# A vision-transformer stack on one core: six phases in one order, the attention of one image pair beside the projection and MLP of the other pair

## The chip, the core and the metric

The kernel runs on one core of a Trainium2 chip. The metric is the device time of one execution in microseconds (us). Three executions of the kernel before gave a median of 682.43 us (679.1 to 685.9). A core has TensorE (PE, matrix products, results in PSUM), VectorE (DVE), ScalarE (ACT), GpSimd (POOL) and SyncE (SP), which here issues all DMAs. Each engine runs its own instructions in the order in which they were written; between engines there are only semaphores.

## The reference

Input: 4 images of 16 x 16 tokens with 192 channels, float32. Three transformer layers and a spectral layer follow each other:

```python
def layer(x):                      # layers 0, 1, 2
    y = layernorm(x)
    q, k, v = split(y @ wqkv + b)  # 12 heads
    s = q @ k.T * scale + rel_h(q) + rel_w(q)     # decomposed relative positions
    x = x + softmax(s) @ v @ wproj + bproj
    return x + gelu(layernorm(x) @ w1 + b1) @ w2 + b2   # 192 -> 768 -> 192
def spectral(x):                   # last
    f = rfft2(x); f = block_mlp(f)  # relu between, softshrink behind
    return irfft2(f) + x
```

Layers 0 and 2 have 12 heads of 16 channels and windows of 14 x 14: of an image, one window of 196 tokens is whole, and the 60 tokens at its edge lie in three windows filled up with padding tokens, whose keys and values count. Layer 1 has 12 heads of 48 channels over all 256 tokens of an image.

## The kernel before

It works on all four images (1024 tokens, eight tiles of 128 rows in X) and finishes a layer before the next begins: layernorm (DVE, the root on ACT), PE transposes into XT, q and k for 96 channels at a time, the relative terms, 12 heads of attention, projection, second layernorm, `up` with gelu on ACT, `down`, the next layer. The spectral layer closes it.

**One head.** Scores with position terms and masks are one product: SP builds for each head the operands QA and KA in a ring of slots (6 slots in layers 0 and 2, one tile of 128 rows; 4 slots in layer 1, two tiles), 3 or 6 DMAs per head (step `aug`: q with its rounding remainder, k, relative terms). Rows that never change (one-hot keys, masks) are laid once per layer (`load_constants`, L643). PE computes `max` units, DVE reduces them to row maxima, PE transposes the maxima (`maxT`), DVE copies them to NR, SP writes them into the last rows of QA (two DMAs, L726), and with them PE computes the transposed `scores` units, ACT takes the exponential into PT, PE multiplies by V into the O banks (`pv`), DVE and POOL divide.

**The order** is one list of steps, made by `all_steps`; every engine walks through it and issues what it has to do in each step, so the list fixes each engine's program and SP's queue. In `windowed_attention` (layers 0 and 2) and `whole_attention` (layer 1) maxima are taken ahead of the scores by some heads, the q, k and relative units of later chunks lie between the heads, and `attention_steps` adds projection and MLP at the end, with the second half of the images' layernorm beside the first half's products. All matmuls but the transposes go through one helper line, L1171, so operand names tell them apart: XT,WQKV (q, k), WQKV,XT (v), QD,RB and XNOS,RB (relative terms), QA,KA (maxima), KA,QA (scores), PT,V (pv), OT,WP (projection), XT,W (`up`), W,HT (`down`). An f32 matmul appears as two records in the trace. Layernorm in DVE's program:

```python
link(nc.vector.reciprocal(RSTD[:, 4 * u:4 * u + 4], STD[:, 4 * u:4 * u + 4]))
```

after ACT's square root of the variance (L859), which needs its own function table; so do exp and gelu.

Of the kernel before, what the change touches and what calls it, by code (L numbers as in the profile page):

```python
# [7 lines left out]
F32R = mybir.dt.float32r  # L23
ALU = mybir.AluOpType
# [6 lines left out]
TILES = NT // 128  # L31
CK = C // 2
HEADS, HALF = 12, 6
# [8 lines left out]
EDGES = 2 * BORDER  # L42
FIRST_EDGE = NB * INNER
PAD_KEYS = INNER - (IMG - EDGE) ** 2
FIRST_PAD = FIRST_EDGE + EDGES
PROBS = 2 * FIRST_EDGE + 2 * EDGES + 4 * EDGES
# [5 lines left out]
SHRINK = 0.01  # L52


class Layer:


    def __init__(self, index, head_dim, window, eps, gelu):
# [7 lines left out]

# [7 lines left out]
        self.npad = PAD_KEYS if self.pads else 0  # L74
        self.keys = NT + self.npad
        self.pc = self.npad // 2
        self.vtiles = 2 * NB + 2 if self.pads else TILES


        self.tiles = 1 if head_dim == 16 else 2  # L80
        self.ring = 6 if head_dim == 16 else 4
        parts = 2 if self.tiles == 1 else 1
        self.rel_row = 3 * head_dim if self.tiles == 1 else head_dim
        self.mask_row = self.rel_row + 2 * parts * window

        self.max_row = 126
        self.rows = 128
        self.depth = (self.rows,) * self.tiles
        self.aug_dmas = 3 if self.tiles == 1 else 6

        self.score_banks, self.unit_banks = ((2, 3, 4), (5,)) if self.tiles == 1 else ((2, 3), (4, 5))
        self.units = 6 if self.pads else 4
        self.pv_heads = 4 if self.pads else 2
        self.pv_steps = 5 if self.pads else 4
        self.max_units = 6 if self.pads else 4
        self.max_rows = 120 if self.pads else 128
        self.max_cols = 20 if self.pads else 16
        self.max_dmas = 2 if self.pads else 1
        self.per_pair = 4 if self.tiles == 1 else 8
# [3 lines left out]
          Layer(2, 16, 14, 1e-6, ACT.Gelu)]  # L103

# [6 lines left out]

def key_constants(L):

    w, parts = L.win, 2 if L.tiles == 1 else 1
    n = L.keys if L.pads else TOK
    hot = np.zeros((w, parts, 2, n), np.float32)
    masks = np.zeros((L.max_row - L.mask_row, n), np.float32)
    ones = np.ones((2, n), np.float32)

    def place(j, kh, kw):  # L120
        hot[w - 1 - kh, :, 0, j] = 1
        hot[w - 1 - kw, :, 1, j] = 1

    if not L.pads:
        for j in range(TOK):
            place(j, *divmod(j, IMG))
        hot = hot.transpose(2, 0, 1, 3)
# [3 lines left out]
    for b in range(NB):  # L131
        for i, (y, x, window) in enumerate(border()):
            j = edge_keys(b // 2).start + b % 2 * BORDER + i
            place(j, y % w, x % w)
            masks[b % 2 * 3 + window, j] = 1
    j = FIRST_PAD
    real = IMG - w
    for kh in range(w):
        for kw in range(w):
# [7 lines left out]
            j += 1  # L147
    return np.ascontiguousarray(np.concatenate([hot.reshape(-1, n), masks, ones]))


def query_masks():

    m = np.zeros((LAYERS[0].max_row - LAYERS[0].mask_row, NT), np.float32)
    for b in range(NB):
        for i, (_, _, window) in enumerate(border()):
            j = edge_queries(b // 2).start + b % 2 * BORDER + i
            m[:WINDOWS, j] = -BIG
            m[b % 2 * 3 + window, j] = 0
# [3 lines left out]


def edge_queries(k):
    return slice(FIRST_EDGE + k * EDGES, FIRST_EDGE + (k + 1) * EDGES)


def edge_keys(k):
    at = FIRST_EDGE + k * (EDGES + PAD_KEYS)
    return slice(at, at + EDGES)  # L170

# [5 lines left out]


def pad_keys_of(pc):
    half = PAD_KEYS // 2  # L180
    return slice(FIRST_PAD + pc * half, FIRST_PAD + (pc + 1) * half)
# [16 lines left out]
class Count:  # L198


    def __init__(self, nc, ctx, name, per_layer, step=1):
# [208 lines left out]
def _build(nc, ctx, io, out):  # L410
# [84 lines left out]
    def per(f):  # L495
        return [f(L) for L in LAYERS] + [0]
# [991 lines left out]
```

## Time and profile before

| what | value |
|---|---|
| median of three executions | 682.43 us (679.1 to 685.9) |
| profiled execution: span, instructions | 688.5 us, 9874 |
| PE busy | 590.2 us, 86% |
| DVE / ACT / POOL busy | 300.5 / 221.0 / 119.5 us |
| first scores of layer 0 | 54.2 us |
| scores of layer 0 end; its MLP ends about | 137; 202 us |
| layer 1: first maxima; scores | 237.7; 251 to 400.5 us |
| layer 2: scores | 503 to 585.6 us |
| spectral layer | 643 to 688.5 us |

PE's 86% is the busy time of pipelined matmuls at the clock they were granted; a stretch at half clock looks as busy as one at full clock with twice the work. The page's row PEclk, in tenths of full speed for 40 slices of 17 us, tells them apart. The chain of waits names, step by step back from the last instruction, what the time went to.

### The profile page before, as it was taken

The numbers are of one execution on the slowest core, as the hardware profiler recorded it, in microseconds if no ns is written. First come the engines' busy times: TensorE is split into PE (matmuls) and PEld (weight loads), VectorE is DVE, ScalarE is ACT, GpSimd is POOL, SyncE is SP. The second block draws the span as 40 slices with busy tenths as digits, with TensorE's granted clock in tenths as the row PEclk, the third lists the DMA queues.
The fourth block names the chain that finished last, engine by engine and source line by source line (L and its number), as shares of the span: only waits on it lengthen the run. The fifth ranks groups of instructions, "written<-read, shape, count | busy, mean of one in ns | idle before, by whom it ended". The sixth has DMA issues, their size and how long they took to land.

```text
span 688.5 us, 9874 instructions
## 1 busy us (share of the span) xinstructions
PE 590.2 (86%) x3696; PEld 431.0 (63%) x3696; DVE 300.5 (44%) x824; ACT 221.0 (32%) x437; POOL 119.5 (17%) x179
## 2 busy tenths in 40 slices
PE   7986778789989998898987899998876776999997
PEld 5655646674667666475755686666566465746777
DVE  4566628561133343344443544126566385510123
ACT  3314425524242133143342333134143255242120
POOL 5102001102003203050531114201020011030021
PEclk7897678788999999799999899999986788889999
DMA  5772433145215255408255232601623431120001
GB/s 154 179 153 55 94 78 64 39 110 123 59 36 127 41 112 126 101 1 170 60 111 120 50 96 67 150 11 33 139 69 79 89 69 38 35 59 0 1 0 47
DMA packets 21829, 54.13 MB, mean 79 GB/s; under 512 B 4642, under 2 KB 10522, under 8 KB 21686
## 3 DMA queue, kind: packets, MB, share of 16 engines
q1 hardware_dynamic: 21782, 53.50, 34.2%
q8 instruction: 30, 0.49, 0.3%
q14 instruction: 17, 0.14, 0.1%
HBM read 10.94 MB, written 0.79 MB: 17 GB/s over the span
## 4 chain that ended last, share of the span: by engine, by line
PE 64%; DVE 13%; SPq 9%; DMA 7%; issue 4%; ACT 3%; DVEq 0%; ACTq 0%
PE PS L1171 62%; DVE NM L1067 4%; DMA QA<-NR 4%; DMA QA<-REL 3%; SPq L704 3%; SPq L714 3%; PE PS L1187 2%; SPq L696 2%; SPq L726 1%; DVE REL L1054 1%; ACT REL L902 1%; DVE OT L1104 1%; DVE HL L1080 1%; DVE OT L1102 1%; DVE QHL L1035 1%
## 5 line engine op out<-in xcount | busy, mean ns | idle before, releaser
L1067 DVE TENSOR_REDUCE NM<-PS 98x2 f32<-98x392 f32 (+2 forms) x192 | 105.2, 569 | 109.3 <-PE PS L1171 107.2
L1171 PE MATMUL PS<-QA,KA 128*98 128x196 f32 (+2 forms) x480 | 103.8, 333 | 29.6 <-DMA QA<-NR 19.1
L1171 PE MATMUL PS<-KA,QA 126*98 126x196 f32 (+3 forms) x432 | 101.9, 336 | 28.8 <-DVE NM L1067 16.8
L922 ACT ACTIVATE PT<-PS 98x392 f32<-98x392 f32 (+2 forms) x192 | 94.2, 520 | 98.1 <-PE PS L1171 94.1
L1171 PEld LDWEIGHTS PS<-QA,KA 128*98 128x98 f32 (+2 forms) x480 | 80.6, 218 | 43.2 <-DMA QA<-NR 21.4
L1171 PEld LDWEIGHTS PS<-KA,QA 126*98 126x98 f32 (+3 forms) x432 | 69.5, 206 | 55.3 <-DVE NM L1067 28.2
L1171 PE MATMUL PS<-XT,W 96*128 96x512 f32 x144 | 70.0, 643 | 3.4 <-issue 3.4
L1171 PE MATMUL PS<-XT,WQKV 96*96 96x512 f32 x128 | 66.6, 654 | 4.7 <-issue 3.8
L1171 PE MATMUL PS<-PT,V 128*32 128x196 f32 (+2 forms) x672 | 56.8, 391 | 0.0
L1054 DVE TENSOR_TENSOR REL<-PS,REL 32x512 fp32r<-32x512 f32 (+5 forms) x64 | 28.4, 478 | 57.6 <-ACT REL L902 57.5
L1171 PE MATMUL PS<-W,HT 128*128 128x192 f32 x288 | 48.7, 328 | 4.7 <-ACT HT L943 4.7
L1171 PEld LDWEIGHTS PS<-W,HT 128*128 128x128 f32 x288 | 46.6, 190 | 9.6 <-ACT HT L943 9.6
L1171 PEld LDWEIGHTS PS<-XT,W 96*128 96x128 f32 x144 | 28.9, 206 | 37.6 <-issue 36.9
L823 POOL TENSOR_TENSOR OT<-XNOS,OT 128x512 f32<-128x512 f32 x18 | 22.8, 1274 | 151.2 <-DVE OT L1104 151.2
L902 ACT ACTIVATE REL<-PS 32x512 fp32r<-32x512 f32 (+5 forms) x64 | 25.1, 433 | 66.0 <-PE PS L1171 53.5
L1129 DVE TENSOR_TENSOR X<-X,PS 128x192 f32<-128x192 f32 x24 | 8.5, 354 | 84.7 <-PE PS L1171 84.7
L943 ACT ACTIVATE HT<-PS,COL 128x512 f32<-128x512 f32 x36 | 24.0, 685 | 53.4 <-PE PS L1171 53.4
L1171 PEld LDWEIGHTS PS<-XT,WQKV 96*96 96x96 f32 x128 | 21.6, 179 | 29.3 <-issue 29.2
L1171 PEld LDWEIGHTS PS<-PT,V 128*32 128x32 f32 (+2 forms) x672 | 27.5, 132 | 15.2 <-issue 2.5
L1171 PE MATMUL PS<-QD,RB 96*32 96x64 f32 x384 | 35.1, 253 | 1.5 <-DVE NR L1091 1.5
L1171 PEld LDWEIGHTS PS<-QD,RB 96*32 96x32 f32 x384 | 30.9, 117 | 6.9 <-DVE NR L1091 2.8
L804 POOL CAST QHL<-QD 96x1024 fp32r<-96x1024 f32 x6 | 6.2, 1035 | 154.6 <-ACT QD L882 90.5
(96 smaller groups left out, 674.7 us busy)
## 6 DMA issues: line engine op xcount, KB each, us to landing
QA<-QHL SPq DMA_DIRECT2D x36, 192.0 KB
KA<-KHL SPq DMA_DIRECT2D x24, 228.0 KB
QA<-REL SPq DMA_DIRECT2D x24, 224.0 KB
QA<-QHL SPq DMA_DIRECT2D x12, 384.0 KB
KA<-KHL SPq DMA_DIRECT2D x12, 384.0 KB
KA<-PT SPq DMA_DIRECT2D x12, 380.0 KB
W<-in_w SPq DMA_DIRECT2D x6, 576.0 KB, 5.2
QA<-REL SPq DMA_DIRECT2D x24, 128.0 KB
```

What stands on the lines that cost most here:

```text
L696: sp.dma_start(raw(dst), raw(src)).then_inc(aug_in[s].sem, 16)
L704: sp.dma_start(raw(dst), raw(src)).then_inc(aug_in[s].sem, 16)
L714: sp.dma_start(raw(dst), raw(src)).then_inc(aug_in[s].sem, 16)
L823: nc.gpsimd.tensor_tensor(o, OS[:, k, :], o, ALU.mult).then_inc(o_done.sem, 1)
L902: ins = nc.scalar.activation(dst, src, ACT.Copy)
L922: nc.scalar.activation(dst, src, ACT.Exp).then_inc(probs_done.sem, 1)
L943: nc.scalar.activation(m["HT"][:, i, u * 512:(u + 1) * 512], PS[:, bank, :], L.gelu, bias=COL[n][:, b1:b1 + 1]).then_inc(gelu_done.sem, 1)
L1054: ins = nc.vector.tensor_tensor(lo, src, hi.bitcast(F32), ALU.subtract)
L1067: nc.vector.tensor_reduce(dst, src, AX.X, ALU.max, negate=True).then_inc(max_done.sem, 1)
L1129: nc.vector.tensor_tensor(X[:, i, :], X[:, i, :], PS[:, bank, 0:C], ALU.add).then_inc(x_end.sem, 1)
L1171: return nc.tensor.matmul(dst, lhsT, rhs, start=start, stop=stop, skip_group_check=loose)
L1187: last = nc.tensor.transpose(PS[0:CK, bank + k, t * 128:(t + 1) * 128], XN[:, 4 * u + t, k * CK:(k + 1) * CK], IDN[:, :])
```

## The change

The images are split into two pairs (HB = 2), and the three layers into six phases, layer x pair: phase 0 and 1 are layer 0 of pairs 0 and 1, 2 and 3 layer 1, 4 and 5 layer 2. While the attention of phase p runs, unit by unit, the steps of `beside(p)` are put between its units: the tail of phase p-1 (projection, layernorm, `up`, gelu, `down`: the other pair) and the head of phase p+1 (layernorm, transposes, q, k, relative terms: again the other pair, next layer or same). They fill the first 75% of the attention's units (FILL). Each layer loads its weights once, in its first phase. Other edits go with it:

- Masks and operands are for two images; maxima are no longer split in two parts, one row (127) of QA holds them.
- Relative terms: per unit 64 matmuls of 32 x 32, to four column groups of PE in turn; 18 units in all, 2304 records instead of 640 records of 64 columns.
- Layernorm: 1/sqrt on DVE by an integer guess and three Newton steps, 12 small linked operations, instead of ACT's Sqrt and DVE's reciprocal.
- `up` leaves PSUM by an Identity on ACT; gelu then works in place over 128 x 1536, twice per phase, with one table load before it and one behind, inside the attention (13 loads in all, 6 before).
- PSUM: two banks for maxima, two for scores, one for O, three for everything beside (four, two and two before).
- At a change of layer kind (phase 1 to 2, 3 to 4) the constants of the ring (12 DMAs) are laid once all scores of the phase before are done, then `prelude`: the ring's `aug` DMAs (24, or 18) and the first heads' maxima, all ahead of the new phase's first scores.
- Matmul instructions go from 2370 to 3286, SP's DMAs from 280 to 481.

```diff
+def tail_steps(p):
+    out = [(("proj", 0, 0), 1.5), (("proj", 1, 0), 1.5), (("ln", 1, 0), 5.0), (("turn", 1, 0), 3.0)]
+    out += [(("up", m, 0), 1.5) for m in range(FM)]
+    out += [(("gelu", 0, 0), 0), (("gelu", 1, 0), 4.0)]
+    return out + [(("down", k, 0), 2.0) for k in range(2)]
...
+def beside(p):
+    out = []
+    if p:
+        out += [((p - 1, *step), d) for step, d in tail_steps(p - 1)]
+    if p % 2 == 0:
+        out.append(((p, "weights", 0, 0), 0))
+    if p == 5:
+        out += [((4, *step), d) for step, d in spectral_steps(0)]
+    if p + 1 < 6:
+        out += [((p + 1, *step), d) for step, d in head_steps(p + 1)]
+    return out
...
+FILL = [0.75] * 6
...
+def ordered():
+    out = [(0, *step) for step, _ in head_steps(0)]
+    out += prelude(0)
+    for p in range(6):
+        L = PHASES[p].L
+        if p and PHASES[p - 1].L is not L:
+            out += [(p, "constants", 0, 0), *prelude(p)]
+        out += second_chunk(p)
+        out += [(p, "v", t, 0) for t in range(L.vtiles)]
+        slots, extra = attention_slots(p), beside(p)
+        whole, at, placed = sum(d for _, d in extra) / FILL[p], 0.0, []
+        for step, d in extra:
+            placed.append((at / whole * len(slots), step))
+            at += d
+        for j, slot in enumerate(slots):
+            out += slot
+            while placed and placed[0][0] < j + 1:
+                out.append(placed.pop(0)[1])
+        out += [step for _, step in placed]
+        out += [(p, "pv", L.groups - 1, k) for k in range(L.pv_steps)] + [(p, "norm", 0, 0)]
+    out += [(5, *step) for step, _ in tail_steps(5)]
+    return out + [(5, *step) for step, _ in spectral_steps(1)]
...
+                link(nc.vector.tensor_scalar(VAR[:, :], MV[:, :, 1], L.eps, None, ALU.add))
...
+                for _ in range(3):
+                    link(nc.vector.tensor_tensor(SQ[:, :], RSTD[:, :], RSTD[:, :], ALU.mult))
+                    link(nc.vector.scalar_tensor_tensor(SQ[:, :], SQ[:, :], -0.5, VAR[:, :], ALU.mult, ALU.mult))
+                    link(nc.vector.scalar_tensor_tensor(RSTD[:, :], SQ[:, :], 1.5, RSTD[:, :], ALU.add, ALU.mult))
...
+            elif step == "constants":
+                sp.wait_ge(*scores_psum.at(p - 1, HEADS * PHASES[p - 1].L.units - 1))
+                lay_constants(ph)
+            elif step == "weights":
...
+                load_weights(L)
+                if p == 0:
+                    load_wqkv(1)
+                    for k in (1, 2):
+                        sp.dma_start(COL[k][:, :], io[f"col{k}"]).then_inc(col_in[k].sem, 16)
+                        load_columns(k)
...
+                for y in range(IMG):
+                    at = y % L.win
+                    for j in range(4):
+                        chunk, axis = divmod(j, 2)
+                        tokens, to = image(Q[rows, chunk, :]), image(PS[32 * j:32 * j + 32, bank[0], :])
+                        last = mm(to[:, :, :, y] if axis else to[:, :, y, :], RB[n][rows, axis, at:at + 16, :],
+                                  tokens[:, :, :, y] if axis else tokens[:, :, y, :], True, True)
```

**PE around the second layernorm of layer 0.** A row is one or several equal matmuls in PE's program: out<-weights,moving, rows x columns of it. Before, behind the projection (OT,WP), all images:

```order
L1171 MATMUL PS<-WP,OT 128x192 x24
L1187 MATMUL PS<-IDN,XNOS 96x128 x8
L1171 MATMUL PS<-XT,W_0 128x512 x4
L1187 MATMUL PS<-IDN,XNOS 96x128 x8
L1171 MATMUL PS<-XT,W_0 128x512 x8
L1171 MATMUL PS<-W_0,HT 128x192 x24
L1171 MATMUL PS<-XT,W_0 128x512 x12
L1171 MATMUL PS<-W_0,HT 128x192 x18
```

In the changed kernel, phase 1: the same layernorm (its transposes are IDN,XN x8, `up` is XT,W), with the attention of the other pair around it; the projection's second half (WP,OT x12) stands five rows above the first row:

```order
L1122 MATMUL PS<-QA,KA 98x196 x2
L1214 MATMUL PS<-IDN,NM 6x120
L1122 MATMUL PS<-KA,QA 98x196 x2
L1122 MATMUL PS<-QA,KA 98x196 x2
L1122 MATMUL PS<-KA,QA 98x196 x2
L1140 MATMUL PS<-IDN,XN 96x128 x8
L1122 MATMUL PS<-QA,KA 120x120 x3
L1122 MATMUL PS<-KA,QA 120x312
L1122 MATMUL PS<-QA,KA 98x196 x2
L1214 MATMUL PS<-IDN,NM 6x120
L1122 MATMUL PS<-KA,QA 98x196 x2
L1122 MATMUL PS<-XT,W 128x512 x2
```

Between the projection and the transposes lie 17 small attention matmuls (maxima QA,KA, scores KA,QA and one transpose of maxima), and between the transposes and the first `up` nine, where before the transposes followed the projection directly and `up` of the other half lay behind them.

**SP at the change from layer 0 to layer 1.** A row is one DMA. Before, behind the last rows of maxima (QA<-NR), while PE is at projection and MLP:

```order
L726 DMA QA<-NR 2x2x120
L731 DMA W_0<-in_w_0 96x1536
L732 DMA W_0<-in_w_0 128x1152
L641 DMA WQKV<-in_wqkv 96x3456
L673 DMA RB<-in_rb 96x124
L673 DMA VB<-in_vb 128x576
L673 DMA B_1<-in_b_1 128x192
L673 DMA COL<-in_col 128x26
L647 DMA KC<-in_kc 80x256
L658 DMA KA<-KC 80x4x256
L658 DMA KA<-KC 32x4x256
L662 DMA QA<-KC 46x4x256
```

In the changed kernel, behind the last rows of maxima of phase 1, with the first DMA waiting for the last scores:

```order
L676 DMA QA<-NR 1x15x8
L615 DMA KA<-KC 80x2x256
L615 DMA KA<-KC 32x2x256
L619 DMA QA<-KC 47x2x256
L615 DMA KA<-KC 80x2x256
L615 DMA KA<-KC 32x2x256
L619 DMA QA<-KC 47x2x256
L615 DMA KA<-KC 80x2x256
L615 DMA KA<-KC 32x2x256
L619 DMA QA<-KC 47x2x256
L615 DMA KA<-KC 80x2x256
L615 DMA KA<-KC 32x2x256
```

The weights are gone from this place, the constants have moved behind the last scores of the phase, and the `aug` DMAs of four heads follow them (six per head) before any maxima of layer 1.

**SP in phase 0.** In the changed kernel, from the row of head 2 (the first rows) on:

```order
L674 DMA QA<-NR 1x4x98
L676 DMA QA<-NR 1x15x8
L600 DMA WP<-in_wp 128x576
L601 DMA W<-in_w_0 96x1536
L602 DMA W<-in_w_0 128x1152
L591 DMA WQKV<-in_wqkv 96x3456
L693 DMA COL<-in_col 128x26
L594 DMA RB<-in_rb 96x124
L595 DMA VB<-in_vb 128x576
L596 DMA B_1<-in_b_1 128x192
L693 DMA COL<-in_col 128x18
L594 DMA RB<-in_rb 96x116
```

Behind these loads (ten of twelve are shown) stand, in the same queue, the operands of head 6 and the row of maxima of head 3. Before, the loads of the next layer stood behind the last rows of a layer's attention.

## Rows read from the trace of the kernel before

**Rows 1.** The page: span, busy time, and the granted TensorE clock in 40 slices
```profile
span 688.5 us, 9874 instructions
...
PE 590.2 (86%) x3696; PEld 431.0 (63%) x3696; DVE 300.5 (44%) x824; ACT 221.0 (32%) x437; POOL 119.5 (17%) x179
...
PEclk7897678788999999799999899999986788889999
```

**Rows 2.** Chain that ended last, shares of the span by engine
```profile
PE 64%; DVE 13%; SPq 9%; DMA 7%; issue 4%; ACT 3%; DVEq 0%; ACTq 0%
```

**Rows 3.** Stretches of 10 us: PE, PEld, DVE, ACT, POOL busy (instructions), granted clock, DMA
```profile
80.00:90.00 10.00, 2.34 (x17) 1.77 (x16) 3.33 (x11) 2.31 (x5) 0.00 (x0) 0.84 0.99 189
...
130.00:140.00 10.00, 7.99 (x57) 6.07 (x61) 1.89 (x8) 6.51 (x13) 1.26 (x1) 0.50 0.52 148
...
630.00:640.00 10.00, 9.22 (x32) 5.29 (x31) 0.34 (x1) 3.17 (x5) 0.00 (x0) 1.00 0.00 0
```

**Rows 4.** Timeline of PE: start, length, operation, count; dense work
```profile
170.74 8.07 PE L1171 MATMUL PS<-W,HT 128*128 128x192 f32 x48 [0.78 <-ACT HT L943]
178.64 10.46 PE L1171 MATMUL PS<-XT,W 96*128 96x512 f32 x24
...
215.60 8.76 PE L1171 MATMUL PS<-WQKV,XT 96*128 96x288 f32 x35
```

**Rows 5.** Timeline of PE: attention of layer 1 and of layer 2
```profile
262.80 1.08 PE L1171 MATMUL PS<-QD,RB 96*32 96x64 f32 x16
...
399.81 1.01 PE L1171 MATMUL PS<-QA,KA 128*128 128x256 f32 x7
400.75 3.67 PE L1171 MATMUL PS<-PT,V 128*64 128x256 f32 x32
...
545.15 0.40 PE L1171 MATMUL PS<-KA,QA 126*120 126x312 f32 x1
```

**Rows 6.** Timeline of PE: four narrow matmuls side by side
```profile
590.14 0.58 PE L1171 MATMUL PS<-PT,BV 96*32 96x120 f32 x16
590.56 0.38 PE L1171 MATMUL PS<-PT,V 120*32 120x120 f32 x8
590.76 0.58 PE L1171 MATMUL PS<-PT,BV 96*32 96x120 f32 x16
```

**Rows 7.** Chain, pieces in order of time (start, length): row of maxima, layer 0
```profile
81.92 1.10 SPq L696
...
83.08 1.36 SPq L704
...
84.53 0.83 SPq L714
...
85.42 0.72 SPq L726
...
86.19 4.29 DMA QA<-NR
...
133.19 1.65 DMA QA<-NR
```

**Rows 8.** Timeline of SP: constants laid into the ring's slots
```profile
21.54 0.81 SPq L654 DMA_DIRECT2D QA<-PT  x1
22.39 1.38 SPq L653 DMA_DIRECT2D KA<-PT  x1
```

**Rows 9.** Groups by shape on DVE and ACT: busy us, mean ns of one
```profile
L996 DVE TENSOR_SCALAR XNOS<-X,MV,RSTD 128x192 f32<-128x192 f32 x48 | 16.6, 409 | 0.4
...
L980 DVE BATCH_NORM_STATS2 STAT<-X 128x6 f32<-128x192 f32 x48 | 13.6, 345 | 3.1 <-DMA X<-in_x 3.1
...
L987 DVE RECIPROCAL RSTD<-STD 128x4 f32<-128x4 f32 x12 | 2.1, 178 | 27.7 <-ACT STD L859 27.7
...
L863 ACT ACT_TABLE_LOAD x6 | 7.7, 1283 | 0.1
```

**Rows 10.** DMA issues: KB each, median us to landing
```profile
WQKV<-in_wqkv SPq DMA_DIRECT2D x1, 1296.0 KB, 11.4
```

More of the change, by code:

```diff
@@ new lines, in attention_slots @@
+def attention_slots(p):
+    L = PHASES[p].L
+    slots = {(h, k): [(p, "scores", h, k)] for h in range(HEADS) for k in range(L.units)}
+    joined = p + 1 < 6 and PHASES[p + 1].L is L
+    for h in range(HEADS):
+        g, first = h // L.per_group, h % L.per_group == 0
+        if first and g:
+            for k in range(L.units):
+                slots[h, k].append((p, "pv", g - 1, k))
+            slots[h, L.units - 1].append((p, "copy_o", g - 1, 0))
+            slots[h + 1, 0].append((p, "inverse", g - 1, 0))
+            slots[h + 1, L.units - 1].append((p, "divide", g - 1, 0))
+        m = h + L.ahead
+        where = (p, m) if m < HEADS else (p + 1, m - HEADS) if joined else None
+        if where:
+            for k in range(L.units):
+                slots[h, k].append((where[0], "max", where[1], k))
+            late = (h + 1, 0) if h + 1 < HEADS else (h, L.units - 1)
+            slots[late].append((where[0], "maxT", where[1], 0))
+        a = h + L.ring
+        if a < HEADS:
+            slots[h, L.units - 1].append((p, "aug", a, 0))
+        elif joined and a - HEADS < L.ring:
+            slots[h, L.units - 1].append((p + 1, "aug", a - HEADS, 0))
+    if not L.pads:
+        for i in range(1, 3):
+            work = [(p, *step) for step, _ in unit_steps(i)]
+            at = range(0, 4) if i == 1 else range(4, 12)
+            for j, step in enumerate(work):
+                k = at[j * len(at) // len(work)]
+                slots[k // 2, k % 2].append(step)
+    return [slots[h, k] for h in range(HEADS) for k in range(L.units)]
@@ L405, in build, with all_steps @@
+BANKS = {"turn": 2, "q": 1, "k": 1, "rel": 1, "maxT": 1, "proj": 1, "up": 1, "down": 1, "fwd": 1, "s1": 1, "s2": 1,
+         "inv": 1}
+def all_steps():
+    taken = 0
+    for p, step, i, u in ordered():
+        n = BANKS.get(step, 0) if step != "v" else 1 if PHASES[p].L.pads else 2
+        banks = [DENSE[(taken + k) % len(DENSE)] for k in range(n)]
+        taken += n
+        yield PHASES[p], step, i, u, banks
 def build(nc, io, out):
@@ L582, in values, with split_free @@
+    def split_free(p, c):
+        L = PHASES[p].L
+        rooms = 1 if L.pads else 2
+        if c >= rooms:
+            return chunk_heads(p, c - rooms)
+        if not p:
+            return []
+        if new_layer(p):
+            return [wait for b in range(1, 3) for wait in chunk_heads(p - 1, PHASES[p - 1].L.chunks - b)]
+        return chunk_heads(p - 1, L.chunks - rooms + c)
     def values(L, t, h):
-        return mem[L.index]["V"][0:v_rows(L, t), t, h * L.vcol:h * L.vcol + L.slot]
+        rows = EDGES if L.pads and t == 2 * HB else 128
+        return V[L.index][0:rows, t, h * L.vcol:h * L.vcol + L.slot]
@@ L1207, in _ @@
+                        last = mm(PS[0:rows, bank[g], 0:wide], tokens, WQKV[n][:, k, cols], k == 0, k == 1)
                 last.then_inc(v_psum.sem, 1)
             elif step in ("q", "k"):
[L1209 to L1210 removed]
+                part = int(step == "k")
+                pe.wait_ge(*wqkv_in[n].at(0, 0))
                 permuted = part and L.pads
[L1212 removed]
```

1725 lines of the change are left out of this document (776 added, 949 removed).

## Prediction

> **What bounds the kernel now.** I read the page first. PE is busy 86% of 688.5 us [rows 1], and the granted-clock row says that part of this is slow work: slices at 0.6 to 0.8 lie where attention is. The chain's shares come next: PE 64%, and the rest in small waits (DVE 13%, SP's queue 9%, DMA 7%, issue 4%) [rows 2]. The windows show the two kinds of stretch. At 80 to 90 us PE has 2.34 us of work in 10 while DMAs are busy 99%; at 130 to 140 us PE is busy 7.99 us but the granted clock is 0.50, that is 1.2 GHz; at 630 to 640 us, in the MLP's dense products, it is busy 9.22 us at 1.00, 2.4 GHz [rows 3]. So layers 0 and 2 leave PE idle or at half clock in attention, and it is dense elsewhere. That is the only thing that laying MLP beside attention can win back; the products themselves stay.
>
> **PE's work at full clock.** Starts per record: 192 columns 0.168 us (8.07/48), 512 columns 0.436 us, 288 columns 0.25 us [rows 4]; in attention 256 columns 0.14 us at most, and 0.115 us each in pv (3.67/32), a 64-column relative term 0.068 us; a lone scores product of 312 columns shows 0.40 us to its modelled end [rows 5], in a row I charge 0.135 by its columns, so 0.135 to 0.40. With the records of each step, per pair: projection 4 us (8 in layer 1), transposes 1, `up` 10.3, `down` 7.8, so a tail is 23 (27 behind layer 1); q and k 1.7 a chunk; a head of layers 0 and 2 has 1.3 of scores and maxima, of layer 1 2.0; pv 6 and 10 per phase; v 3.3 and 7.8.
>
> The **relative terms** have no row of their kind: 32 columns, four column groups in turn, 128 records per unit. Nearest are four narrow matmuls of 120 columns side by side: 24 records start in 0.62 us, 26 ns each [rows 6]. Four of them start every 104 ns, which is what 120 columns take at the pace of the 512-column record (0.436 x 120/512 = 0.102), so four share the time of one. Low end: 32 columns so, 27 ns for four, 0.9 us per unit. High end: 26 ns per record, 3.3 us. I take 1.5, nearer to the low end, as this row shows nothing slower than the array. 18 units are 27 us (17 to 60), against 640 records x 0.06 = 41 before. The Trainium skill ("TensorE: Matmul & The Clock Gate", Wait — 56ns, not 53.3ns?) says that start to start never falls below about 25 ns, however few the columns. By that rule the sum would be 33 us higher; no row here has a group short enough to decide it, so it is rival C.
>
> All of it: about 471 us at full clock before, 465 after. **By phase** after: before the first scores 17, then 37, 61.5, 91, 93, 63.5, 60.5, and 41 behind the last pv.
>
> **The timeline, phase by phase** (first scores to first scores), each PE work plus what stands bare:
>
> - Start: 45 us. Half the tokens are normalised and projected before the first scores, which stand at 54 now; constants are laid as before.
> - Phase 0: 69. 37 work. SP issues twelve loads, some 3.4 MB, ahead of the maxima row of head 3; 1296 KB take 11.4 us to land [rows 10] while DMAs are already full [rows 3], so 3.4 MB are up to 30 us, of which heads 0 to 2 cover about half: 16. Light heads 7: three operand DMAs and two row DMAs cost SP 1.10, 1.36, 0.83 and twice 0.72 us [rows 7], 3.5 to 4.7 per head at half the tokens, where PE has 1.3 to 3. The head's boundary with v 3, half clock in light heads 6.
> - Phase 1: 100.5. 61.5 work. Layernorm is now 4 x 0.345, 4 aggregations and 12 small linked operations at 0.16 to 0.2 (the nearest is the 128x4 reciprocal at 178 ns), then 4 x 0.409: 5.3 us [rows 9]. Between projection and transposes PE has 17 attention products, some 1.6 us, in its order; behind the transposes nine, some 1 us, while ACT copies XT. So each of the two layernorms of this phase leaves 4 to 4.5 us bare, with the copies 11 in all. What is queued behind the waiting transposes on PE are the maxima and scores of two heads, and DVE and ACT wait for those. Last heads 4, clock 2. Then the **layer change**: 12 constants, 0.81 to 1.38 us each [rows 8] at more tokens, so 0.65 here, 8 us; 24 operand DMAs at 0.62, 15 us; the row, 0.7 and 2.3 to land. 26, of which the last pv and the first maxima cover 4: 22.
> - Phase 2: 107. 91 work; the last nine heads hold less filler, and a head of layer 1 costs SP six operand DMAs, a row and its landing (3.7 + 0.7 + 2.3 = 6.7 us) against 5 to 6 of PE: 9. Weights on the same queue 5, clock 2.
> - Phase 3: 120. 93 work, 3 last heads, 21 layer change (12 + 18 DMAs), 3 clock.
> - Phase 4: 86. 63.5 work, 11 for two layernorms, 5 light heads, 3 weights, 3 clock.
> - Phase 5: 75.5. 60.5 work, 6 layernorm, 5 spectral chain of pair 0, 4 last heads and clock.
> - End, nothing beside it: 66. Norm 3, projection 6, layernorm 5.9, transposes and copies 3.3, `up` 12, gelu with its table load 3.5, `down` 9, spectral layer of pair 1 23.
>
> 669 us. Half clock in stretches not counted above: 6. That makes a span of 675, against 688.5. The median of the runs shown, 682.4, is 6 below the profiled span, so 669.
>
> Costed at nothing: the 13 table loads of 1283 ns [rows 9], since ACT has 221 us of work in 688 and the exponentials of two banks wait; without that cover 12 x 1.3 = 15 us. The row shows 0.1 us idle before a load, and none shows a wait behind one. The Trainium skill ("ScalarE: Activation LUTs", What ACT_TABLE_LOAD costs) adds a drain of about 1380 ns to each switch, which would make the uncovered sum twice that.
> The row of the landing ranges from 4.29 us, DMAs full, to 1.65 us [rows 7]; I used 2.0 to 2.3, as fewer constants travel.
>
> **Rivals.**
>
> *A, the covers work better.* The list is uneven, but two maxima and two score banks let PE run on, and the bare stretches I added (7, 11, 9, 11, 6, clock 20) overlap. For it: the chain has 36% beside PE, and all of it could be hidden. Against: each engine has a fixed order. It gives 669 less 35 to 40: 630.
>
> *B, slower: the row of maxima sits behind the operands in SP's queue.* In about 30 heads with little filler (most of phase 0, the ends of all) the time of a head is SP's issues plus the landing plus DVE's reduce. Pads or not, a pair now needs the same number of DMAs per head as four images did: 481 issues against 280. If the landing is 4 to 5 us, as the 4.29 us row, and not 2, each such head costs 2 to 3 us more: 75 us, 740. It decides from a landing of about 3 us, where the gain is gone. For it: SPq and DMA hold 16% of the chain with half the heads' DMAs per token; light heads also sit at the lower clock. Against: the late row of 1.65 us.
>
> *C, narrow records.* At 26 ns a record the relative terms cost 60 us, not 27. They lie in the filler, where PE is the bound: 669 + 30 = 699.
>
> *D, it doesn't overlap:* each filler step makes PE wait for DVE or ACT, and attention waits behind it. Two or three more waits of 3 us in 12 tails and heads, 60 us: 725.
>
> **How the numbers follow.** Forecast (650 to 690) 0.30, A 0.22, B 0.23, C 0.14, D 0.11. A measurement of this kernel can tell about 1%. Faster by over 1% (below 675.6): A, six in ten of the forecast and a part of C mixed with A, 0.50 in all. Within 1%: 0.12. Slower: B, D, most of C, the rest of the forecast, 0.38. The time is that of the forecast, 669. Range 612 to 745: A's lower half below, B's centre above; the relative terms' ends (-10, +33), the landing's (-10, +75), table loads (+15) and the 312-column product (+0.27 x 36 x 0.5 = 5) lie inside.
>
> **What would show it.** First scores at about 45 us. In phase 0 a hole of some 16 us on PE between 50 and 70 us with DMAs near 1.0. Two holes of about 20 us, one at the end of phase 1 (near 215) and one at the end of phase 3 (near 440), with SPq and DMA into KA and QA on the chain. In phases 1 and 4 PE's transposes IDN,XN waiting for DVE's XN 4 us each time. Relative units of 64 matmuls: their span says 0.9, 1.5 or 3.3. Last scores at about 600 us. The forecast is wrong if landing of QA<-NR is over 3 us in most heads (B), if the waits on XN or XT are over 6 us each (D), or if PEclk stays at 0.5 in phases 0, 1, 4 and 5 although filler is there: at half clock their 220 us of work would be the bound for up to 50 us more.

## The result and the profile after

The changed kernel takes **795.55 us** (median of 4 runs, 790.65 to 796.73) against 683.12 us before (679.1 to 685.9): ratio 1.167, 95% interval 1.159 to 1.174. It is 17% slower; the forecast was 669, and the range (612 to 745) does not hold it.

The page of the changed kernel, the three lines that answer to [rows 1]:

```profile
span 792.7 us, 13858 instructions
...
PE 601.9 (76%) x5444; PEld 434.8 (55%) x5444; DVE 314.9 (40%) x846; ACT 224.7 (28%) x420; POOL 125.1 (16%) x154
...
PEclk8666756698856999979989997678986779997799
```

PE is busy 12 us longer in a span 104 us longer, and the granted clock is lower in the slices of attention. The chain's shares, against [rows 2]:

```profile
PE 59%; DVE 16%; SPq 8%; DMA 7%; issue 5%; ACT 5%; DVEq 0%; POOL 0%; ACTq 0%
```

The same engines, with DVE and ACT up by 3 and 2 points. Four windows, columns as in [rows 3]:

```profile
50.00:60.00 10.00, 0.00 (x0) 0.00 (x0) 1.77 (x11) 0.00 (x0) 0.58 (x3) 0.50 0.78 162
100.00:110.00 10.00, 8.81 (x270) 7.04 (x272) 4.03 (x13) 2.57 (x7) 0.00 (x0) 0.50 0.36 78
230.00:240.00 10.00, 0.00 (x0) 0.00 (x0) 0.00 (x0) 0.00 (x0) 0.00 (x0) 0.50 0.45 134
550.00:560.00 10.00, 10.00 (x41) 5.62 (x40) 2.92 (x6) 5.31 (x10) 0.00 (x0) 1.00 0.20 44
```

At 50 to 60 PE does nothing while weights travel; at 100 to 110 it is busy 8.81 us at 1.2 GHz; at 230 to 240 it stands still at the first layer change; at 550 to 560, with the MLP of one pair beside the attention of the other, it is busy all the time at 2.4 GHz. That last window is what the change was to make of the whole span.

One thing on names, for all rows below. In the views of the trace the moving operand stands first and the weights second, so `QA,KA` are the scores and `KA,QA` the maxima. The code says the same: the maxima use QA as weights and read 127 rows, without the row of maxima, and the rows `KA,QA 127*98` have 127. The list of names ahead of the prediction has the two the other way round; the sums do not depend on it.

What PE waited for (us in total, times, longest wait), the first rows:

```profile
PE PS L1214 <- DVE NM L1043: 54.4, 29, 18.3
PE PS L1122 <- issue: 46.0, 10, 24.0
PE PS L1122 <- DMA QA<-NR: 20.3, 8, 7.7
PE PS L1122 <- DVE NM L1043: 13.9, 9, 4.6
PE PS L1122 <- DVE V L1001: 13.4, 4, 6.1
PE PS L1122 <- ACT HT L896: 10.9, 5, 3.6
```

Before, PE was idle for 98 us in all, and 12 of them stood ahead of the transpose of maxima (there L1264). Now it is 191 us, and this one transpose (L1214), waiting for DVE's row maxima, is the largest entry at 54. "Issue" is mostly the layer changes, 24.0 and 9.9 us.

I split both spans with windows of 1 us: PE's idle time, its busy time times the granted clock (work), and the rest of its busy time. The rest is what running below 2.4 GHz would cost if all of PE's work took half as long at twice the clock; the relative terms below do not, so it is an upper bound.

| us | idle | work at full clock | below full clock | span |
|---|---|---|---|---|
| before | 98 | 530 | 60 | 688.5 |
| after | 191 | 511 | 91 | 792.7 |

And by phase, from the first exponential of one to that of the next, against the forecast's terms:

| | start | 0 | 1 | 2 | 3 | 4 | 5 and end |
|---|---|---|---|---|---|---|---|
| forecast | 45 | 69 | 100.5 | 107 | 120 | 86 | 141.5 |
| measured | 44.8 | 96.2 | 119.1 | 123.7 | 144.7 | 110.3 | 153.9 |

### The profile page after: what moved, and what is told of

Read it like the earlier page. It is cut to its first block, busy times and chain, and to the rows that moved or that the text cites. A ratio compares the mean times of both kernels' runs of the same rounds, so it can differ in the third digit from the quotient of the medians.

```text
span 792.7 us, 13858 instructions
## 1 busy us (share of the span) xinstructions
PE 601.9 (76%) x5444; PEld 434.8 (55%) x5444; DVE 314.9 (40%) x846; ACT 224.7 (28%) x420; POOL 125.1 (16%) x154
## 4 chain that ended last, share of the span: by engine, by line
PE 59%; DVE 16%; SPq 8%; DMA 7%; issue 5%; ACT 5%; DVEq 0%; POOL 0%; ACTq 0%
PE PS L1122 56%; DVE NM L1043 3%; DMA QA<-NR 3%; DMA COL<-in_col 2%; DVE STAT L954 2%; PE PS L1140 1%; DMA QA<-KC 1%; SPq L615 1%; PE PS L1214 1%; DVE XN L973 1%; DVE QHL L1016 1%; ACT HT L896 1%; SPq L654 1%; SPq L648 1%; DVE RSTD L965 1%
## 5 line engine op out<-in xcount | busy, mean ns | idle before, releaser
L872 ACT ACTIVATE PT<-PS 98x392 f32<-98x392 f32 (+2 forms) x192 | 96.2, 513 | 319.1 <-PE PS L1122 318.6
L1043 DVE TENSOR_REDUCE NM<-PS 98x2 fp32r<-98x392 f32 (+2 forms) x192 | 108.1, 572 | 146.4 <-PE PS L1122 145.0
L1122 PE MATMUL PS<-QA,KA 128*98 128x196 f32 (+2 forms) x528 | 124.8, 348 | 28.3 <-DMA QA<-NR 20.3
L1122 PE MATMUL PS<-KA,QA 127*98 127x196 f32 (+3 forms) x432 | 105.5, 344 | 48.5 <-issue 33.9
L1122 PEld LDWEIGHTS PS<-KA,QA 127*98 127x98 f32 (+3 forms) x432 | 72.8, 217 | 69.8 <-issue 50.2
L1214 PE MATMUL PS<-IDN,NM 120*6 120x120 f32 (+1 forms) x72 | 22.9, 318 | 54.4 <-DVE NM L1043 54.4
L1122 PE MATMUL PS<-W,HT 128*128 128x192 f32 x288 | 52.6, 343 | 10.9 <-ACT HT L896 10.9
L771 POOL TENSOR_TENSOR OT<-OS,OT 128x512 f32<-128x512 f32 x18 | 23.0, 1276 | 205.7 <-DVE OT L1061 205.6
L1122 PE MATMUL PS<-Q,RB 32*32 32x32 f32 (+1 forms) x2304 | 37.7, 225 | 5.0 <-issue 4.1
L1214 PEld LDWEIGHTS PS<-IDN,NM 120*6 120x6 f32 (+1 forms) x72 | 5.9, 83 | 61.5 <-DVE NM L1043 61.5
L1122 PEld LDWEIGHTS PS<-Q,RB 32*32 32x32 f32 (+1 forms) x2304 | 34.8, 126 | 8.6 <-issue 7.5
L1122 PE MATMUL PS<-WP,OT 128*128 128x192 f32 x192 | 36.0, 351 | 3.0 <-DVE OT L1075 3.0
L1122 PEld LDWEIGHTS PS<-WP,OT 128*128 128x128 f32 x192 | 35.1, 210 | 4.2 <-issue 4.2
```

The lines of the kernel that those rows point to most:

```text
L771: nc.gpsimd.tensor_tensor(OT[:, i, :], OS[:, :], OT[:, i, :], ALU.mult).then_inc(o_done.sem, 1)
L872: nc.scalar.activation(dst, src, ACT.Exp).then_inc(probs_done.sem, 1)
L1043: nc.vector.tensor_reduce(dst, src, AX.X, ALU.max, negate=True).then_inc(max_done.sem, 1)
L1122: return nc.tensor.matmul(dst, lhsT, rhs, start=start, stop=stop, skip_group_check=loose)
L1214: nc.tensor.transpose(PS[0:cols, bank[0], 0:rows], NM[n][0:rows, h % 2, 0:cols].bitcast(F32), IDN[0:rows, 0:rows]).then_inc(maxT_psum.sem, 1)
```

## The experiments

Times are medians of four runs. The changed kernel has 795.5.

**e1_tail_first**: is the interleaving the loss?

```diff
-            placed.append((at / whole * len(slots), step))
+            placed.append((0 if step[0] == p - 1 else at / whole * len(slots), step))
```

> Against the changed kernel (795.5 us). The whole tail (projection, layernorm, up, gelu, down) of the other pair stands behind the first scores of a phase instead of between its heads; the next head keeps its places. Theory 1: laying the tail beside attention does hide waits and keeps the clock up, and the loss comes from elsewhere (two pairs, layer changes, waits of VectorE); then without it each of phases 1 to 5 loses some 10 us: about 845. Theory 2: the interleaving itself costs as much as it hides, since layernorm and splits stand in VectorE's order ahead of the row maxima; then 780 to 800.

Measured 872.6 us, ratio to before 1.277 (1.266 to 1.287): 77 us slower than the changed kernel. PE's timeline in phase 1 shows what the overlap had covered:

```profile
138.66 4.16 PE L1122 MATMUL PS<-WP,OT 128*128 128x192 f32 x24
147.94 2.08 PE L1140 MATMUL PS<-IDN,XN 128*96 128x128 f32 x8 [5.12 <-DVE XN L973]
150.89 13.03 PE L1122 MATMUL PS<-XT,W 96*128 96x512 f32 x24 [0.87 <-ACT XT L817]
```

The transposes wait 5.12 us for the layernorm with nothing to do. Theory 1 holds, with more than the 50 us I gave it: laying the tail beside attention helps. The two-pair kernel without it is 188 us slower than the kernel before.

**e2_cols**: the columns of layers 1 and 2 loaded at the start.

```diff
-        sp.dma_start(COL[0][:, :], io["col0"]).then_inc(col_in[0].sem, 16)
+        for k in range(3):
+            sp.dma_start(COL[k][:, :], io[f"col{k}"]).then_inc(col_in[k].sem, 16)
...
-                        sp.dma_start(COL[k][:, :], io[f"col{k}"]).then_inc(col_in[k].sem, 16)
```

> Only the two small column loads (COL 1 and 2) move from behind the 3.4 MB of phase 0 to the start; all other loads stay where they are. VectorE head-of-line theory: the hole of 18.3 us in phase 0 is VectorE waiting for these columns with row maxima queued behind; it shrinks to under 6 us and the time falls by 12 to 15 us, plus up to 5 for the clock: about 778. Queue theory (what I forecast: the row of maxima of head 3 waits on SP's queue and the DMA engines behind 3.4 MB): the hole stays over 12 us and the time within 4 us of 795.

Measured 786.4 us, 9 less. In the changed kernel PE's program stood like this in phase 0, and the chain below it says why:

```profile
45.89 0.34 PE L1122 MATMUL PS<-QA,KA 128*98 128x196 f32 x2
64.53 0.36 PE L1214 MATMUL PS<-IDN,NM 120*6 120x120 f32 x1 [18.30 <-DVE NM L1043]
```

```profile
45.21 13.10 DMA COL<-in_col
```

DVE stood at its small bias product (SKB) for a load of some 10 KB behind 3.4 MB. The layernorm of the next pair and then the row maxima that PE's transpose wanted came next in DVE's program. With early columns:

```profile
45.28 0.34 PE L1122 MATMUL PS<-QA,KA 128*98 128x196 f32 x2
51.12 0.36 PE L1214 MATMUL PS<-IDN,NM 120*6 120x120 f32 x1 [5.50 <-DVE NM L1043]
```

The hole is 5.50 us instead of 18.30, what the layernorm alone takes. Behind it a second one opens, 2.69 us long: the row of maxima of head 3, which lands 6.79 us after its issue. That is the wait that I had forecast; in the changed kernel the longer hole covers it.

**e5_split_pool**: the split of q in layers 0 and 2 on GpSimd.

```diff
-            if (step == "qs" and not L.pads) or step == "ks":
+            if step in ("qs", "ks"):
...
+                if step == "qs" and L.pads:    # GpSimd, the same seven operations
...
-            elif step == "qs" and L.pads:      # VectorE
```

> Against the changed kernel (795.5 us). The split of q into rounded and rest for layers 0 and 2 (8 blocks of 5.8 us on VectorE, some waiting there for operand DMAs of the other pair) goes to GpSimd, same place in the order. If VectorE's order is what couples the pairs (row maxima queued behind the split): the holes of 9.8 us at 85, 5.8 at 586 and parts of 3.6 and 6.1 at the pair boundaries go, 12 to 20 us less, about 780. If TensorE would wait for the split's result anyhow: within 4 us of 795.

Measured 766.8 us, 29 less, more than either theory said. DVE's timeline of the changed kernel at such a place:

```profile
82.46 1.09 DVE L1043 TENSOR_REDUCE NM<-PS 98x2 fp32r<-98x392 f32 x2
88.95 1.17 DVE L1011 CAST QHL<-Q 96x392 fp32r<-96x392 f32 x3 [5.40 <-DMA QA<-REL]
90.16 2.71 DVE L1014 CAST QHL<-QHL 96x512 fp32r<-96x512 f32 x1
92.79 1.88 DVE L1016 TENSOR_TENSOR QHL<-Q,QHL 96x392 fp32r<-96x392 f32 x3
94.59 0.47 DVE L1043 TENSOR_REDUCE NM<-PS 120x1 fp32r<-120x312 f32 x1
```

The split of the *next* phase's q waits 5.40 us until the operands of the last heads of *this* phase have been copied out of the same room (QHL), then works 5.6 us; the reduce at 94.59, of this phase's attention, waits for all of it, and PE with it for 9.80 us. In the profiled executions 20 of the 29 us lie in phase 0 (96.2 to 76.0 us).

**e6_ln_parts**: each layernorm in four steps, in different units.

```diff
-    out = [(("ln", 0, 0), 5.0), (("turn", 0, 0), 3.0)]
+    out = [(("ln", 0, k), 1.7) for k in range(4)] + [(("turn", 0, 0), 3.0)]
...
```

> Each layernorm is cut into four steps (sums, aggregation and guess, Newton, normalising) that lie in different units of the attention; nothing else. VectorE theory: the holes of 4.6 to 5.4 us behind the five layernorms of phases 1, 4 and 5, and the smaller ones of 2 and 3, shrink to under 2 us each: 12 to 20 us less, about 780. Rival: the time comes back at the transposes, which now come later: within 5 us of 795.

Measured 781.4 us, 14 less. In the changed kernel PE stops here, in phase 1:

```profile
147.46 0.40 PE L1122 MATMUL PS<-QA,KA 128*98 128x196 f32 x2
153.18 0.36 PE L1214 MATMUL PS<-IDN,NM 120*6 120x120 f32 x1 [5.32 <-DVE NM L1043]
```

and DVE meanwhile does this:

```profile
147.04 0.56 DVE L1043 TENSOR_REDUCE NM<-PS 98x2 fp32r<-98x392 f32 x1
147.52 1.13 DVE L954 BATCH_NORM_STATS2 STAT<-X 128x6 f32<-128x192 f32 x4
...
151.49 1.25 DVE L973 TENSOR_SCALAR XN<-X,MV,RSTD 128x192 f32<-128x192 f32 x4
152.65 0.47 DVE L1043 TENSOR_REDUCE NM<-PS 120x1 fp32r<-120x312 f32 x1
```

The whole layernorm stands between two reduces of the same head.

**e8_three**: the three mends together.

> Early columns, split of q on GpSimd and layernorm in four parts together. If these three are the same kind of wait (attention of one pair held up in VectorE's order by work of the other) and add up: 795 less 9 less 16 less 16, about 755, idle of TensorE down from 190 to 145. If something else takes their place (the layer changes, thin attention at half clock): 775 to 785. Either way it stays over 10% slower than the kernel before, so that the rest must lie in the clock and the layer changes.

Measured 750.3 us: 45 less, of 52 for the three apart. PE's idle time is 143 us, down from 191. They are one kind of wait, and they nearly add up; a part of the difference is that e6 also shortens the hole of phase 0, from 18.3 to 11.7 us, which e2 takes away.

**e7_fill**: `FILL = [0.75, 1.0, 0.75, 1.0, 0.75, 1.0]`.

> FILL is 1.0 instead of 0.75 in phases 1, 3 and 5, so the other pair's steps reach to the last head. If the bare last heads matter (half clock, waits on the row of maxima): 5 to 12 us less, about 787. If they don't (last heads of phase 1 take 1.7 us each as it is): within 4 us of 795, or slower by some, because the next head's last steps then delay the layer change.

Measured 799.0 us (792.4 to 802.5): no difference. The bare last heads of phases 1, 3 and 5 cost nothing that later filler won.

**e3_act_queue**: the constants of the layer changes issued by ScalarE.

```diff
+            elif step == "constants":          # ScalarE's program
+                act.wait_ge(*scores_psum.at(p - 1, HEADS * PHASES[p - 1].L.units - 1))
+                lay_constants(ph, nc.scalar)
...
```

> At both layer changes the 12 constant DMAs are issued by ScalarE, so that SP goes straight to the operand DMAs. If SP's issuing sets the hole: 8 to 14 us less at each change, about 773. If the DMA engines' transfer of the constants sets it (the last constant landed 11.75 us after its issue): under 4 us each, about 790.

Measured 794.8 us: no difference. The chain in ScalarE's version, at the first change (ACTq is its DMA issue):

```profile
216.94 10.58 ACTq L592
...
236.16 10.40 DMA QA<-KC
```

One issue takes 10.58 us, and the last constant lands 10.40 us after its own. SP's operand copies have gone ahead meanwhile, and in the last 8 us nothing moves but constants (last columns: granted clock, DMA share, GB/s):

```profile
238.00:242.00 4.00, 0.00 (x0) 0.00 (x0) 0.00 (x0) 0.00 (x0) 0.00 (x0) 0.50 0.07 22
242.00:246.00 4.00, 0.00 (x0) 0.00 (x0) 0.00 (x0) 0.00 (x0) 0.00 (x0) 0.50 0.07 22
```

The transfers set the change, not SP's issues. But the DMA engines are not full either: a share of 0.07 is about that of one of the 16. The changed kernel has the same 22 GB/s from 230 to 234 us. An estimate from it: each of the four copies QA<-KC (47 rows, 94 KB) takes 4.3 us at that pace, which is the length of SP's long issues (3.53 and 4.02 us), and four of them 17 us. That it is these copies, and that a copy of another shape would go faster, is not shown: no run changed them.

**e4_warm**: unused 128x128 products in PE's holes.

```diff
...
+            if step == "constants":
+                keep_warm(90 if p == 2 else 36)
...
```

and 60 in the hole of phase 0, 16 behind each layernorm.

> Unused 128x128 products fill TensorE's holes: 90 and 36 at the layer changes, 60 in the hole of phase 0, 16 ahead of the first transpose of maxima behind each layernorm from phase 1 on. Clock theory (the holes cost more than their length, because TensorE comes out of them at 1.2 GHz and runs on so): mean granted clock rises from 0.825 to 0.87 or more and the time falls by 15 to 25 us, to about 775. Rival: the clock is low because of the thin attention stretches themselves, the holes have no after-effect: clock outside the holes unchanged, time 795 to 810, since the products take TensorE's time where they last longer than the hole.

Measured 794.3 us, granted clock 0.875 instead of 0.825, idle down from 191 to 133 us, but work up from 511 to 585 by the added products: no time gained. The windows at the first change:

```profile
226.00:230.00 4.00, 4.00 (x38) 4.00 (x38) 0.00 (x0) 0.00 (x0) 0.00 (x0) 1.00 0.27 78
238.00:242.00 4.00, 0.00 (x0) 0.00 (x0) 0.00 (x0) 0.00 (x0) 0.00 (x0) 0.69 0.65 188
242.00:246.00 4.00, 2.43 (x10) 2.16 (x11) 1.39 (x2) 0.00 (x0) 0.00 (x0) 0.50 0.65 190
```

The products ended 5.6 us early and the clock was back at 0.50 when the work came, so this run alone leaves the after-effect of that hole open.

**e9_v_first**, on e8_three: the value products ahead of the constants at the layer changes.

```diff
+            out += second_chunk(p)
+            out += [(p, "v", t, 0) for t in range(L.vtiles)]
             out += [(p, "constants", 0, 0), *prelude(p)]
-        out += second_chunk(p)
-        out += [(p, "v", t, 0) for t in range(L.vtiles)]
+        else:
+            out += second_chunk(p)
+            out += [(p, "v", t, 0) for t in range(L.vtiles)]
```

> Base: the kernel with the three mends (750.3 us). At the two layer changes the value products (11.1 us at half and full clock in phase 2's trace, 3.3 and a key chunk in phase 4) move in the order from behind to ahead of the constants, so TensorE does them while the constants and operands travel. Layer-change theory (a bare hole of 24 and 8.5 us with work behind it that needs nothing of it): 10 to 11 us less at the first change and 4 to 5 at the second, about 735. If the DMAs set the change and the first scores come no earlier because VectorE must evict the values first: under 5 us less, about 746.

Measured 746.1 us, 4 less; the ranges touch (741.5 to 748.8 against 748.6 to 755.8). In the profiled executions the first change shortens by 8 us (last to first exponential 45.6 to 37.5), and phase 2 behind it is 5 us longer.

Such figures of single phases need care from here on. Phase 0 is the same program in e8, e9 and e11, and it took 68.2, 73.4 and 68.1 us: the row of maxima behind the weights landed after 9.14, 13.02 and 9.53 us. A difference of 5 us in one phase of one trace says little.

**e10_thin**, on e9_v_first: three unused products ahead of each transpose of maxima in thin attention.

```diff
+            if step == "maxT" and L.pads and (p == 0 or i >= 9):
...
+                for _ in range(3):
+                    mm(PS[:, spare[0], 0:128], WARM[:, :], WARM[:, :], True, True)
```

> Base: e9_v_first. Three unused 128x128 products (0.66 us at full clock) ahead of each transpose of maxima in all heads of phase 0 and in heads 9 to 11 of phases 1, 4 and 5: 21 places, 14 us of products. Clock theory (thin attention runs at 1.2 GHz because TensorE waits in between, and filling the waits brings it to 2.4): phase 0 gets shorter although it has more to do, granted clock there from about 0.65 to over 0.85, time 5 to 12 us under the base. Rival: the granted clock there is not the bound, the waits are: time 0 to 14 us over the base.

Measured 748.3 us against 746.1: no difference. Two windows of phase 0 without and with the products:

```profile
90.00:100.00 10.00, 9.75 (x190) 7.57 (x190) 4.23 (x11) 3.58 (x11) 0.04 (x1) 0.50 0.35 78
100.00:110.00 10.00, 8.36 (x57) 6.50 (x60) 5.51 (x13) 3.40 (x7) 1.23 (x1) 0.50 0.34 75
```

```profile
90.00:100.00 10.00, 8.72 (x219) 6.25 (x209) 2.33 (x7) 2.41 (x8) 0.00 (x0) 0.80 0.32 69
100.00:110.00 10.00, 7.92 (x75) 6.24 (x68) 6.63 (x16) 4.83 (x12) 1.27 (x1) 0.86 0.25 56
```

The clock goes from 0.50 to 0.80 and 0.86. Over the span, what lies below full clock falls from 94 to 75 us, work rises from 515 to 533 and idle time from 138 to 140: what the clock gave, the added products took. Whether a clock that rose without them would shorten the kernel is not shown by it.

**e11_gelu**, on e9_v_first: `(("gelu", 1, 0), 8.0)` instead of 4.0.

> Base: e9_v_first. The weight of the second gelu in the plan is 8 instead of 4, so that `down` stands one to two units later. The waits for gelu (3.3, 3.3, 3.6, 4.4 us in the changed kernel, PE at `down` <- ACT HT) shrink in phases 2 and 3: 5 to 10 us under the base. If ACT's table loads and gelu are waited for by the exponentials as well, or the steps behind get squeezed: within 4 us of the base.

Measured 748.8 us against 746.1: no difference. Phases 2 and 3 became shorter (131.5 to 120.9 and 138.8 to 132.1 us), phases 1, 4 and 5 with the end longer by 22 together.

**e12_weights_late**, on e9_v_first: the loads of phase 0 behind the next pair's head.

> Base: e9_v_first (746.1 us). The 3.4 MB of phase 0 are issued behind the last step of the next pair's head instead of ahead of the row of maxima of head 3, which landed 13.0 us after its issue there. Queue theory (the transfer of the weights holds that row): hole of 9.5 us gone, 8 to 12 us less, about 736. Rival: the loads now delay another row of maxima in heads 9 to 11 by as much: within 3 us of the base.

Measured 750.6 us against 746.1, 4.5 more; the ranges touch (748.7 to 753.0 against 741.5 to 748.8). There is no gain, as the rival said, though the loss is over its 3 us. The row of maxima behind the weights, in phase 0 of e9 and at the end of it in e12:

```profile
49.54 13.02 DMA QA<-NR
```

```profile
102.46 9.37 DMA QA<-NR
```

Phase 0's last exponential comes at 99.1 instead of 106.7 us, the first of phase 1 at 118.4 instead of 117.4. In both places the 3.4 MB hold up the small row that stands behind them.

**e13_half_prelude**, on e12: only the first two (three) slots laid ahead of the first maxima.

```diff
+            first = [step for step in prelude(p) if step[1] != "aug" or step[2] < L.ahead]
+            out += [(p, "constants", 0, 0), *first, (p, "constants", 1, 0)]
+            out += [(p, "aug", h, 0) for h in range(L.ahead, L.ring)]
...
```

> Base: e12_weights_late. At the layer changes only the constants and operands of the first two (three) ring slots are laid ahead of the first maxima, the other half behind the first rows of maxima. If SP's queue and the DMA engines between last scores and first scores set the change: half of the 36 DMAs leave that way, the first change shortens from 37.5 to about 25 us and the second from 24 to about 17: 12 to 18 us less, about 722. If it is only moved (heads 2 and 3 wait as long): under 5 us less.

Measured 760.1 us against 750.6, slower by 9.5. The last constant of the first half, and that of the second:

```profile
196.33 10.72 DMA QA<-KC
```

```profile
219.65 10.51 DMA QA<-KC
```

The first change itself shortens as expected, from 37 to 25 us, but phase 2 behind it grows from 129 to 144. Six DMAs or twelve, the last one lands 10.4 to 11.8 us after its issue (10.4 in e3, 11.75 in the changed kernel); halved, that is paid twice, and both landings are on the chain.

**e14_mended_tail_first**: e13 with the tail in one block.

> Base: e13_half_prelude, with the tail of the other pair laid in one block behind the first scores as in e1_tail_first. In the changed kernel the overlap of the tail was worth 77 us. If it is worth the waits it covers, whatever the mends: 70 to 85 us over the base, about 800. If a good part of those 77 us was waits that the mends took away: 30 to 50 us over the base. Either way it stays 90 us or more over the kernel before, which has no such overlap: the loss then comes with the two pairs and six phases, not with the interleaving.

Measured 839.4 us against 760.1: the overlap is worth 79 us with the mends, 77 without. It does not live on waits that the mends took away. Against the kernel before, e14 is 155 us slower.

## Why the prediction was wrong

**The sum.** The failing step is "The timeline, phase by phase, each PE work plus what stands bare". It was built up from nothing and never laid against the kernel before. There the same prices give 471 of work, and with the 98 idle and 60 below full clock of its trace that makes 629, where the span is 688.5: 59 us were missing, since the work in the windows is 530. After, 46 are missing (511 against 465). Most of them can be named. By operand names, scores and maxima take 147 us of the 511, 1.8 us a head in layers 0 and 2 and 2.5 in layer 1, where I charged 1.3 and 2.0; that is 37 us. The transposes of maxima, 7 us, had no term. My terms for the clock add up to 24 us; measured are 91. My bare terms add up to 186 us; measured idle is 191. So 117.7 us were missing from the span: 67 in the clock, 46 in the work, 5 in the waits. Taken as a difference, the same list would have said that the kernel gets slower: 688.5 + (186 - 98) - 6 = 770. That is still 22 short of the span, 31 for the clock and 5 for the waits, less 14 that the work fell further than I had it.

**Half clock.** I charged it as if filler would lift the clock. The 24 us were guesses of 2 to 6 a phase, against 60 in the trace of before that I had not added up. The 91 lie everywhere: 10 before the first scores, 21 in phase 0, 13 to 15 in each of phases 1, 3, 4 and 5 with the end, 5 in phase 2. The sign that I had named did not show in full: the mean granted clock of phases 0, 1 and 4 and of phase 5 with the end was 0.64, 0.77, 0.81 and 0.90, not 0.5. How much of the 91 is time that the kernel would win back at 2.4 GHz stays open: some 6 of them are relative terms, which take as long at either clock (below), and e4 and e10 raised the granted clock with empty products and came out even.

**The waits, one by one.** The total was right by luck, the parts were not.
- Phase 0's hole: 16 forecast, 18.3 measured, behind the same 3.4 MB; but through DVE's wait for the columns (e2), not through the row of maxima in SP's queue. That wait was there below it, and shorter: PE stood 2.7 us for it in e2, 5.2 in e8, 5.6 in e11 and 9.5 in e9.
- Layernorm: 4 to 4.5 us forecast, 4.6 to 5.4 measured in phases 1, 4 and 5. Yet PE did not wait at its transposes IDN,XN, as I had it, but at a transpose of maxima (5.3 to 5.4) or at maxima whose PSUM bank DVE had not read (4.6). Only at the end, with no attention beside it, did it wait at IDN,XN (5.1). I named who waits behind PE's transposes and did not look at DVE's own order, where the reduces stand behind the twelve small operations.
- The split of q on DVE had no term. Taking it off DVE was worth 29 us (e5), the largest single part of what the runs could win back. It was in the code and in the trace of before, and I had costed only PE and SP of the moved head.
- At the boundary of two phases PE waited for DVE's value tiles (V), 13.4 us in four places; only phase 0 had a term for it, 3 us. A part of this too is the split of q: with it on GpSimd (e5) the time from the last exponential of phase 0 to the first of phase 1 fell from 15.7 to 9.4 us.
- Layer changes: 22 and 21 us forecast, with SP's issues as the price; PE idled 24.0 and 9.9, and last to first exponential took 45.4 and 32.5. The size came out near, the cause was another: SP's issues cost 0.6 to 0.8 us each but for two, which took 3.53 and 4.02, and then comes the landing, which had no term here. The end of the chain at the first change:

```profile
223.86 4.02 SPq L615
...
228.57 11.75 DMA QA<-KC
240.32 2.28 issue
```

- Relative terms: 1.5 us a unit forecast. A unit of 128 records (64 matmuls, two records each) takes 2.1 us at 1.2 GHz (first row, granted clock 0.50) and at 2.4 GHz (second, 1.00):

```profile
101.38 2.12 PE L1122 MATMUL PS<-Q,RB 32*32 32x32 f32 x128
```

```profile
434.87 2.07 PE L1122 MATMUL PS<-Q,RB 96*32 96x32 f32 x128
```

  37.7 us busy in all, 10 more than forecast and 25 less than before (62). Rival C (26 ns a record) is refuted: 16.2 ns. By the rule of the Trainium skill ("TensorE: Matmul & The Clock Gate", Wait — 56ns, not 53.3ns?), that start to start never falls below about 25 ns, a unit would take 3.2 us, an estimate from 128 records. The trace disagrees, for records that go to four column groups in turn; counted by matmul of the program it is 32 ns, and no run here tells which of the two the rule counts.
- Gelu had a term only at the end. Elsewhere it was costed at nothing; PE waited 10.9 us in all for it at `down`, the end included, and in e11 moving `down` away from it won nothing. Table loads inside the attention:

```profile
172.38 1.28 ACT L896 ACT_TABLE_LOAD   x1
173.68 2.86 ACT L896 ACTIVATE HT<-HT 128x1536 f32<-128x1536 f32 x2
176.55 1.28 ACT L899 ACT_TABLE_LOAD   x1
177.84 0.20 ACT L899 ACTIVATE LOADED<-COL 128x2 f32<-128x2 f32 x1
```

  Each load starts 0.02 us behind the activation ahead of it, and the activation behind it 0.01 to 0.02 us after it; so do all twelve inside the kernel. The drain of about 1380 ns that the Trainium skill ("ScalarE: Activation LUTs", What ACT_TABLE_LOAD costs) adds to a switch does not show.
- The row of maxima lands in 1.7 to 1.9 us on the chain, except behind weights (8.3 at 333 us). Rival B is refuted. D came nearest: attention waits behind filler, though on DVE, and at 725 it was priced too low. The waits on XN that were to be its sign stayed under 6 us.

**What stays open.** The best version, e9, is 63 us over before. By the same split it has 138 us idle, 515 of work and 94 below full clock: 39 more idle, 34 more below clock, 15 less work. Known of it: two layer changes (37.5 and 24 us from last to first exponential in e9) that before lay under the MLP, and a phase 0 of 73 us (68 in two other executions) that has only some 12 us of PE's time from the next head beside it. e1 and e14 show that two pairs in six phases with this kernel's other edits cost 188 us (155 with the mends) before the overlap gives 77 to 79 back; how that splits between the pairs and the other edits was not separated. Nor was the slow copy of constants tried in another shape. No version beat the kernel before.

## What to carry to other kernels

Lay the method of a sum against the kernel that you can measure before you trust it on the one that you can't; if it misses by 59 us there, forecast the difference. When two streams are laid side by side on engines that run in order, walk the order of *every* engine: a wait of the filler on VectorE (a late column, a layernorm, a split that waits for a room) stops the attention whose reduce stands behind it, and costs TensorE the whole of it. When a wait ends with a DMA, look at the rate before you move the issue: at the layer change 22 GB/s went while all waited, and moving or halving the issues (e3, e13) won nothing. And an overlap can be worth 77 us and still lose to what had to be changed to get it, here 188.

## What the runs showed of the hardware

- 32x32 f32 products to four column groups in turn: a unit of 128 records took 2.12 us at 1.2 GHz and 2.07 us at 2.4 GHz, 16 to 17 ns a record at either clock.
- Copies inside SBUF of 64 to 160 KB in pieces of 1 KB with a repeated source moved 74 GB/s in one stretch of 4 us and 22 GB/s in the next, while PE stood and waited:

```profile
226.00:230.00 4.00, 0.00 (x0) 0.00 (x0) 0.00 (x0) 0.00 (x0) 0.00 (x0) 0.50 0.26 74
230.00:234.00 4.00, 0.00 (x0) 0.00 (x0) 0.00 (x0) 0.00 (x0) 0.00 (x0) 0.50 0.07 22
```

- The last of them landed 10.4 to 11.8 us after its issue, whether six or twelve were sent, and ScalarE's queue stood up to 10.6 us at one issue.
- A row of 0.5 to 2 KB inside SBUF landed in 1.7 to 1.9 us, and 6.8 to 13.0 us after its issue behind the loads of phase 0; there the same program gave 9.1, 9.5 and 13.0 us in three executions (e8, e11, e9).
- Empty products raised the mean granted clock from 0.825 to 0.875 (e4), and in phase 0 from 0.50 to 0.8 (e10); neither kernel got shorter.
